# The last sums of three of eight chunks on GpSimd, and the stores in another order

## What is computed

```python
x = x + 0.5 * ffn(layernorm(x))
x = x + attention(layernorm(x))
x = x + 0.5 * ffn(layernorm(x))

# ffn(x), the part that matters here:
abel_out = gelu(xn @ abel_w + abel_b)
w_dense  = softmax of the two largest of xn @ moe_gate_w + moe_gate_b, zero elsewhere
h        = gelu(xn @ ew1[e] + eb1[e])              # e = 0..7
moe_out  = sum over e of w_dense[e] * (h @ ew2[e] + eb2[e])
moe_out  = moe_out @ expm(gens[0]) @ expm(gens[1]) @ expm(gens[2])
gate     = sigmoid(concat(abel_out, moe_out) @ gc_w + gc_b)
ffn      = x + abel_out * (1 - gate) + moe_out * gate
```

## Time and profile before

| | before |
|---|---|
| median of the runs shown | 789.28 us (786.37 to 792.46) |
| the profiled execution: its span | 883.8 us, 94.5 us more than the median |
| share of busy time: PE / DVE / ACT / POOL | 77% / 64% / 46% / 55% |
| last result tiles weighted on VectorE (L1799) | 861.35 to 861.97 us |
| last scatter issued on GpSimd (L944) | 863.91 to 864.87 us |
| last instruction of `finish_x` on VectorE ends | 881.11 us |

### The profile page before, as it was taken

How to read it: one execution, slowest core, us unless ns; L and a number is a source line. 1 busy time by engine, 2 the same in 40 slices (tenths; PEclk the granted TensorE clock), 3 DMA queues, 4 the chain that set the end, 5 groups by cost and what they waited for, 6 DMA issues and landing times.

```text
span 883.8 us, 16149 instructions
## 1 busy us (share of the span) xinstructions
PE 683.1 (77%) x4719; PEld 492.3 (56%) x4719; DVE 568.2 (64%) x1922; ACT 410.8 (46%) x931; POOL 485.6 (55%) x588
## 2 busy tenths in 40 slices
PE   1465667979897798997988979999997777838760
PEld 1355656979793354654646545455544466837750
DVE  3675545968767876876767767787673235745538
ACT  2243411545560265664545645556554655615530
POOL 2656554034512666576866768373645466566661
PEclk9968777988898899998999999999997999969985
DMA  8614544744348313023050240302201235233525
GB/s 242 205 48 117 132 123 115 183 112 105 94 113 192 110 31 98 18 65 87 2 130 21 49 103 1 98 17 55 61 13 53 85 78 167 75 93 84 175 96 154
DMA packets 89825, 84.04 MB, mean 95 GB/s; under 512 B 14561, under 2 KB 72556, under 8 KB 89580
## 3 DMA queue, kind: packets, MB, share of 16 engines
q1 hardware_dynamic: 74472, 57.51, 25.8%
q0 software_dynamic: 8800, 19.72, 7.5%
q10 hardware_dynamic: 6468, 5.79, 2.8%
HBM read 43.84 MB, written 31.13 MB: 85 GB/s over the span
## 4 chain that ended last, share of the span: by engine, by line
PE 46%; DVE 15%; another core or an unknown queue 11%; issue 7%; ACT 7%; SPq 5%; ACTq 3%; DMA 3%; POOL 1%; DVEq 0%; POOLq 0%
PE bank L2361 6%; PE bank L2271 6%; PE bank L2401 6%; PE bank L2286 6%; PE bank L2426 6%; SPq L595 4%; DVE mx_of L1923 3%; PE pair L2449 2%; PE bank L2363 2%; ACT beside_parts L1254 2%; DMA qT<-mT_zero 2%; PE pair L2213 2%; PE bank L2246 1%; ACT arena L1326 1%
## 5 line engine op out<-in xcount | busy, mean ns | idle before, releaser
L1326 ACT ACTIVATE arena<-bank 128x512 f32<-128x512 f32 x320 | 184.0, 599 | 175.2 <-PE bank L2401 147.1
L1923 DVE TENSOR_REDUCE mx_of<-bank 128x4 f32<-128x512 f32 x320 | 204.2, 684 | 81.9 <-PE bank L2361 42.9
L2401 PE MATMUL bank<-qT,kZ 128*128 128x512 f32 (+3 forms) x512 | 156.9, 377 | 19.2 <-ACT arena L1326 12.4
L975 POOL TENSOR_SCALAR_AFFINE_SELECT arena<-arena 128x256 f32<-128x256 f32 (+1 forms) x192 | 95.4, 521 | 123.9 <-ACT arena L1326 122.5
L2361 PE MATMUL bank<-kZ,qT 128*128 128x512 f32 x320 | 148.5, 481 | 15.7 <-DVE mx_of L1923 6.2
L2401 PEld LDWEIGHTS bank<-qT,kZ 128*128 128x128 f32 x512 | 95.7, 197 | 49.2 <-ACT arena L1326 24.1
L868 POOL DMA_INDIRECT z_rows<-beside_kZ,place x80 | 78.7, 984 | 51.5 <-DVE place L1685 29.8
L2361 PEld LDWEIGHTS bank<-kZ,qT 128*128 128x128 f32 x320 | 63.1, 200 | 70.7 <-issue 31.4
L885 POOL DMA_INDIRECT sums<-y_rows,y_place x56 | 54.4, 971 | 84.9 <-DMA y_rows<-arena 70.0
L2426 PE MATMUL bank<-arena,vA 128*9 128x512 f32 (+3 forms) x1024 | 92.4, 440 | 5.2 <-POOL arena L975 2.7
L1254 ACT ACTIVATE beside_parts<-bank,hidden_bias 128x128 f32<-128x128 f32 x160 | 45.5, 381 | 69.6 <-remote 44.0
(11 more groups left out here) (286 smaller groups left out, 1306.7 us busy)
## 6 DMA issues: line engine op xcount, KB each, us to landing
arena<-z_rows SPq DMA_DIRECT2D x128, 66.0 KB
qT<-parts SPq DMA_DIRECT2D x42, 128.0 KB
kZ<-parts SPq DMA_DIRECT2D x168, 32.0 KB
y_rows<-arena SPq DMA_DIRECT2D x20, 264.0 KB, 3.3
kZ<-bias_k_r SPq DMA_DIRECT2D x8, 512.0 KB
beside_kZ<-y_rows SPq DMA_DIRECT2D x7, 528.0 KB, 3.9
z_rows<-in_spare SPq DMA_DIRECT2D x4, 528.0 KB
z_rows<-in_spare SPq DMA_DIRECT2D x32, 66.0 KB
```

The costliest lines, as they stand in the source:

```text
L975: g_.affine_select(out=cut, in_=cut, compare_op=ALU.is_ge, fill=0.0, base=0, pattern=[[0, 2], [0, blocks], [1, P]], channel_multiplier=-1) ...
L1326: a_(dst, src, ACT.Exp).then_inc(exp_ok.sem, 1)
L1923: v.tensor_reduce(mx_of[:, queries, :, t, keys], ps_a[n % NA][:, :].rearrange("p (q n) -> p q n", q=NQ), AX.X, ALU.max).then_inc(reduced.s ...
L2401: return mm(outp, kZ[u][:, h, lo:lo + P], qT[u][:, t, lo:SEQ], start=start, stop=True, skip_group_check=(kind != "full"))
```

## The change

GpSimd gets the ends of chunks 2, 4 and 6 of the second layer, after its last scatter and one after the other: `sum_pairs`, then `finish_x`, for each chunk. VectorE keeps chunks 0, 1, 3, 5 and 7, in the same pattern of `finish_x` and a `sum_pairs` two of its own chunks ahead. SP stores in the order 0, 1, 2, 3, 5, 4, 7, 6. ScalarE's eight `gate_tanh` stay in the order 0 to 7; those of chunks 2, 4 and 6 now wait for GpSimd's second step.

```diff
-DVE_SUMS = [(1, c) for c in range(CH)]
-POOL_SUMS = [(0, c) for c in range(CH)]
+LAST_POOL = (2, 4, 6)
+LAST_DVE = tuple(c for c in range(CH) if c not in LAST_POOL)
+DVE_SUMS = [(1, c) for c in LAST_DVE]
+POOL_SUMS = [(0, c) for c in range(CH)] + [(1, c) for c in LAST_POOL]
@@ block.sync
             for c in range(CH):
                 load_sums(c)
-            for c in range(CH):
+            for c in (0, 1, 2, 3, 5, 4, 7, 6):
                 x_done(sp, 1, c)
                 sp.dma_start(ov[:, NT * c:NT * (c + 1), :], xs(c)).then_inc(stored, 16)
@@ block.gpsimd, experts
                 for p in range(PAIRS):
                     beside_experts(p)
                     send_y(p)
+                for c in LAST_POOL:
+                    sum_pairs(1, c)
+                    finish_x(1, c)
@@ block.vector
             experts(1)
-            for c in range(CH):
+            for n, c in enumerate(LAST_DVE):
                 finish_x(1, c)
-                if c + 2 < CH:
-                    sum_pairs(1, c + 2)
+                if n + 2 < len(LAST_DVE):
+                    sum_pairs(1, LAST_DVE[n + 2])
```

## The result

The changed kernel takes 801.75 us (median of 6 runs, 795.71 to 805.63); the kernel before, run beside it, takes 788.85 us (6 runs). The ratio is 1.016, 95% interval 1.0123 to 1.0198: 12.9 us slower (9.7 to 15.6).

A forecast was written before the change was run, and what follows sets the result against it. VectorE was taken to bound the tail. GpSimd's 16.6 us after its last scatter plus 1.9 of turns, VectorE's end at 884.2 and a 2.7 us store gave 886.9 against 883.8: 3.1 us longer, 792.4 us, range 788.0 to 798.0.

The forecast's parts named there:

- The bound of the end: After the last result tiles are weighted, VectorE alone is the bound, ending chunks without a gap, 2.74 us each.
- GpSimd comes later: Rival, chance 0.28: in timed runs GpSimd lags further at the second layer's last scatters; price 5.8 us, 795.1 us.
- What is removed: Three ends of chunks leave VectorE at the kernel's end: 8.2 us, 1.04% of 789.28.
- What is added, alone: GpSimd after its last scatter: 5.54 us per chunk, 16.6 us for three, ending at 881.5 without interference.
- The turns: In the tail, GpSimd and VectorE two-input instructions alternate; GpSimd loses 1.9 us in all and ends at 883.4.
- turns without overlap: Variant of the tail's turns without the 0.14 us overlap: 1.0 us more, some 4.2 us in all.
- The new wait: VectorE's finishes of 5 and 7 wait for ScalarE's tanhs queued behind GpSimd's chunks; VectorE ends at 884.2.
- The stores: At the end, the same eight output stores, none held by a later chunk; 2.7 us kept for the last.
- No turns: Rival, chance 0.14: the tail's additions get along with GpSimd; 789.7 us, no change.
- GpSimd loses at every turn: Rival, chance 0.08: in the tail VectorE keeps the inputs through whole runs of instructions; 797.4 us, over 1% slower.
- the signs by which the text was to be told wrong: GpSimd's instructions all stretched over 0.5 us, its start over 1 us after its last scatter, or anything before 855 us moving.
- The sign of the later GpSimd: In the profile after, a larger gap between the last L1804 and the last L946 would show that rival.

The follow-up runs named there:

- the eleven executions of the table: One profiled execution per row: the kernel before, the change, and edits of either; timed ratios to the kernel before run from 1.0007 to 1.0193.
- the second profile of before: Nothing changed: the unchanged kernel before profiled again, span 784.3 us; ratio 1.0007 (0.9975 to 1.0039).
- the kernel with VectorE early: The whole change, plus tanhs ordered 0, 1, 3, 5, 2, 4, 7, 6 and VectorE's finish of 5 before sums of 7; 1.0193 against before.

## Why the prediction was wrong, step by step

**The bound of the end.** That VectorE alone is the bound from the last weighting on was read from an execution in which GpSimd lagged by 2.9 us. In the eleven executions of the table, all as long as the timed runs, it lags by 13 to 15; in the second profile of before VectorE does chunks 2 to 5 in the lag and is idle for 8.0 us before chunk 6. This is the first step that failed. It stood in the text as the rival "GpSimd comes later", and the sign was in the rows: 97 us of an unknown queue and 31.8 us of waits in the layer, which are 5.1 us in the second profile of before. I gave it 0.28; with a span that is 94.5 us off, the place read from it was worth less than the rival.

**What is removed.** 8.2 us was the work of three chunks, but only chunk 6's 2.74 us lay on the path.

**What is added, alone.** Right: 5.48 us for the first chunk (773.66 to 779.14), and 5.37 where VectorE does nothing beside it (777.84 to 783.21 in the kernel with VectorE early), against 5.54; it starts 0.03 us after the last scatter.

**The turns.** The mechanism was right, the sizes not. GpSimd's three chunks take 17.42 us, 0.8 more than the text's 16.6 and not 1.9: of VectorE's large sums only those of 7 were left, as those of 5 were over. A turn of such a sum costs 0.5 us, not 0.34 to 0.43. VectorE loses far more than the text had for it: in the groups of 4.04, 4.20 and 3.00 us four small additions take 2.6 to 3.7 times their 1.14, because whole GpSimd instructions come between them. The kernel with VectorE early shows that VectorE's loss costs the program nothing here. (The 4.2 us that the text gives for turns without overlap add up to 3.1 + 1.0 = 4.1.)

**The new wait.** Right in kind: VectorE idles behind ScalarE's order, for 11.05 us, though ahead of the finish of 3 and not of 5 and 7 as the text had it. Its end 18.1 us after the last scatter is the rival's 18.0, and by the rival's mechanism: the last three additions follow GpSimd's last instruction (791.08 - 0.14 + 3 x 0.29 = 791.81 against 791.75). Both engines end within 1 us, as said.

**The stores.** "I keep 2.7 us for the last" is the second step that failed, and the costlier one. It took the end of the program as the last addition plus a store. Rows on the closing drain were in the first trace too, and I did not read them; this one ends at 862.0 + 12.1 = 874.1, 9.2 us after the last scatter:

```profile
L189 POOLq DRAIN  x1: 12089/12089/12089, 862.0 to 862.0; - x1
```

That GpSimd "has nothing afterwards" was wrong: its closing drain was under way. With it, the forecast's own sum would have been 883.4 + 9.2 + 0.2 = 892.8 against 883.8, 9.0 us and 798.3; the rival's, with GpSimd's end 883.4 - 864.87 - 1.3 = 17.2 us after the last scatter, 17.2 + 9.2 + 0.2 = 26.6 against its 12.2 + 2.7 = 14.9 for before, 11.7 us and 801.0, near the measured 801.75. By these sums the drain was worth 5.9 us in either case, and the lag 5.8 - 3.1 = 2.7.

**The other rivals.** "No turns" is refuted by the rows above. "GpSimd loses at every turn" comes near in size (797.4) but not in mechanism: it is VectorE that loses. Of the signs by which the text was to be told wrong, neither GpSimd's start, 0.03 us after its last scatter, nor its instructions, of which two in 18 were stretched by about 0.5 us, gave one; none of these signs looks at what follows the last instruction. The sign of the later GpSimd, a gap between the last L1804 and the last L946, did show.

No version faster than the kernel before came out of this. The drain is hidden only while GpSimd ends less than 15.1 - 9.4 = 5.7 us after its last scatter, which is one chunk, and chunk 2 alone relieves VectorE of nothing that it does not do in the lag. More work on GpSimd inside the layer made the program longer; whether less of it would make it shorter is not shown, as no such kernel was run.

## What to carry to other kernels

Before work is moved to an engine because it stands idle at the end, look at what closes the program on it: its last instruction plus its drain must still lie ahead of the old end. Compare the span of a profile with the timed runs first: here one that was 12% longer showed distances between engines that the timed runs did not have, and its rows of waits (GpSimd's 31.8 us for VectorE) named what shrinks when the extra time is gone. And the spare time to fill is that of the engine in the stage concerned: here VectorE had 8 us of it at the end, and GpSimd none in 110 us.

## What the runs showed of the hardware

- GpSimd's closing drain ends 9.2 to 9.3 us after its last instruction, or after the wait ahead of it where that comes later, in all eleven executions of the table, whether the last was a scatter, an addition, a memset or a mere wait, and also after 12.43 us of idling. VectorE's own drain ends with its last instruction (788.9 + 2.9 = 791.8), and SyncE's takes 7 ns. Whether GpSimd's is as long in a kernel without DMAs of its own was not tried. The Trainium skill (VectorE: DVE Perf Modes, The DRAIN you can't avoid) puts the drains of the runtime's own code at about 12 ns on all five engines. Those here stand under a line of the kernel (L189), one for each engine, so whether the page means them is open; SyncE's 7 ns are of that size, GpSimd's 9.2 us are not.
- Beside GpSimd's large instructions, one whole instruction of GpSimd passes between one of VectorE's small two-input additions and the next (4.0 to 4.2 us instead of 1.14 for four). GpSimd loses about 0.5 us at a turn of a large VectorE sum (L905 0.65 instead of 0.19, L907 1.56 instead of 1.04) and 0.1 us or less at a small addition. VectorE's L1786, with one tile of 128x4 as its input, waited too: 0.68 and 1.00 us instead of 0.16, until GpSimd's instruction ended (776.48 against 776.46, 784.26 against 784.24). The Trainium skill (SBUF — State Buffer, Who interferes with whom) says that whoever issues first has the shared ports for the whole instruction; the alternation fits that, since the four additions are four instructions.
- A scatter of 128 rows holds GpSimd for 0.96 us, and the next one starts 0.30 us later, so they come 1.26 to 1.27 us apart at best, however long ago their data was ready.
